# One norm pass, scale and offset in the copy, and a reordered state-space block in a twelve-block kernel

## What is computed

```python
# L1_attn: causal attention with one head
y = layer_norm(x, gamma, beta)          # x is already _layernorm(x)
q, k, v = split(y @ qkv)
p = softmax(causal(q @ k.T / 16))
out = x + (p @ v) @ o_proj

# L3_attn: a state-space layer (512 inner features, 8 heads of 64, state 128)
u_n = layer_norm(u, ln_w, ln_b)
z, x, B, C, dt = split(u_n @ in_proj_w.T)
B, C = rms_norm(B, bnorm_w), rms_norm(C, cnorm_w)
dA = softplus(dt + dt_bias) * -exp(A_log)
y = sum over s <= t of (C[t] . B[s]) * exp(cumsum(dA)[t] - cumsum(dA)[s]) * x[s]   # per head
y = (y + x * D) * silu(z)
out = u + y @ out_proj_w.T
```

## Time and profile before

| | us |
|---|---|
| median of 3 runs | 1470.83 (1466.35 to 1474.09) |
| the profiled execution | 1467.78 |
| its span, first to last instruction | 1466.0 |
| TensorE busy | 1247.5 (85%) |
| VectorE busy | 1132.9 (77%) |
| ScalarE busy | 897.5 (61%) |
| mean granted TensorE clock | 0.940 |

### The profile page before, as it was taken

One profiled execution on the slowest core, in us unless ns is written; L12 is line 12 of the kernel. 1 busy time (PEld: TensorE's weight loads), 2 busy tenths in 40 slices (PEclk: granted clock), 3 DMA queues, 4 the chain that ended last, 5 costly groups with the idle time before them and its releaser, 6 DMA issues. The chain is left out here.

```text
span 1466.0 us, 25694 instructions
## 1 busy us (share of the span) xinstructions
PE 1247.5 (85%) x9953; PEld 852.3 (58%) x9953; DVE 1132.9 (77%) x2075; ACT 897.5 (61%) x1231; POOL 303.2 (21%) x235
## 2 busy tenths in 40 slices
PE   4999998555887899867989999978797999998777
PEld 1677776442334555545756766754684766766444
DVE  6787785588787999937588898955897898897563
ACT  4777776622566787823267777744694777676423
POOL 0000000100241111000005155230461155165020
PEclk9999999887898999977999999999899999999889
DMA  6899997102005999985159998931563899987500
GB/s 241 156 173 188 183 168 124 58 2 99 1 1 101 187 193 187 196 186 137 43 110 196 179 194 168 172 116 34 190 195 90 165 176 180 169 158 128 106 1 8
DMA packets 548297, 196.41 MB, mean 134 GB/s; under 512 B 534624, under 2 KB 535008, under 8 KB 546912
## 3 DMA queue, kind: packets, MB, share of 16 engines
q1 hardware_dynamic: 548192, 195.00, 66.2%
HBM read 60.48 MB, written 0.26 MB: 41 GB/s over the span
## 5 line engine op out<-in xcount | busy, mean ns | idle before, releaser
L654 DVE SCALAR_TENSOR_TENSOR arena<-L_xattn_sm,L_xattn_rr,arena 128x1024 f16<-128x1024 f32 x192 | 278.6, 1491 | 12.1 <-ACT arena L545 12.1
L408 PE MATMUL ps<-ctxT,L_xattn_qk 128*128 128x512 f16 x1152 | 266.2, 381 | 1.9 <-DVE L_xattn_qk L621 1.4
L530 ACT ACTIVATE L_xattn_sm<-L_xattn_sm,L_xattn_mx 128x2048 f32<-128x2048 f32 x96 | 192.3, 2003 | 80.9 <-DVE L_xattn_mx L636 79.7
L545 ACT ACTIVATE arena<-L_xattn_sm,L_xattn_rr 128x1024 f16<-128x1024 f32 x192 | 210.0, 1141 | 5.2
L420 PE MATMUL ps<-arena,ctx 128*128 128x128 f16 x2976 | 188.9, 224 | 20.4 <-DMA arena<-arena 20.4
L420 PEld LDWEIGHTS ps<-arena,ctx 128*128 128x128 f16 x2976 | 177.2, 100 | 35.9 <-DMA arena<-arena 25.3
L408 PEld LDWEIGHTS ps<-ctxT,L_xattn_qk 128*128 128x128 f16 x1152 | 111.2, 98 | 128.4 <-issue 3.8
L636 DVE CUSTOM_DVE_ANT_0 L_xattn_sm<-ps,L_xattn_bias 128x1024 f32<-128x1024 f32 x96 | 117.1, 1220 | 69.2 <-issue 68.9
L636 DVE CUSTOM_DVE_ANT_0 L_xattn_sm<-ps,L_xattn_bias,L_xattn_mx 128x1024 f32<-128x1024 f32 x96 | 123.2, 1283 | 0.8 <-DVE L_xattn_mx L636 0.5
L430 PEld LDWEIGHTS ps<-arena,ctx 128*128 128x128 f16 x1488 | 90.7, 98 | 17.3 <-DMA arena<-arena 0.2
L430 PE MATMUL ps<-arena,ctx 128*128 128x128 f16 x1488 | 98.3, 219 | 0.0
(11 more groups left out here) (534 smaller groups left out, 2148.9 us busy)
## 6 DMA issues: line engine op xcount, KB each, us to landing
L_ffn_ring<-in_L_ffn_experts SPq DMA_DIRECT2D x34, 384.0 KB, 3.5
arena<-in_L_xattn_w SPq DMA_DIRECT2D x36, 320.0 KB, 3.9
arena<-in_L_ffn_experts SPq DMA_DIRECT2D x8, 768.0 KB, 8.6
arena<-in_L_xattn_w SPq DMA_DIRECT2D x6, 640.0 KB, 11.6
arena<-arena SPq DMA_TRANSPOSE x193, 4.5
arena<-in_L_ffn_codes SPq DMA_DIRECT2D x1, 3072.0 KB, 14.2
arena<-in_L_ffn_scales SPq DMA_DIRECT2D x8, 384.0 KB, 24.5
arena<-in_L_attn_w SPq DMA_DIRECT2D x1, 2163.0 KB, 8.8
```

What stands on the lines that cost most here:

```text
L408: last = nc.tensor.matmul(ps[:, at, :], qk[:, h // 2, qp, h % 2, b * P:(b + 1) * P], k.ctxT[:, cp, b, at * 512:(at + 1) * 512], start=(a = ...
L530: nc.scalar.activation(sm[:, u % 2, :], sm[:, u % 2, :], ACT.Exp, bias=mx[:, u % 2, 1:2], scale=-1.0, accum_out=rs[:, u % 2:u % 2 + 1]).th ...
L545: nc.scalar.mul(pp[:, u % 2, 0, at], sm[:, u % 2, at], rr[:, u % 2:u % 2 + 1]).then_inc(s.p_high, 1)
L654: nc.vector.scalar_tensor_tensor(pp[:, u % 2, 1, at], sm[:, u % 2, at], rr[:, u % 2:u % 2 + 1], pp[:, u % 2, 0, at], ALU.mult, ALU.subtrac ...
```

## The change

In both layers the two norms become one pass. The norm of a normed input has the same direction, and its variance follows from the first: with variance v, the two root arguments are v + eps and v(1 + eps) + eps * eps. `ln_twice_vector` takes the statistics once, both roots at once, and writes `twice` first and `once` after it. Scale and offset are held as columns and put into the copy out of PSUM on ScalarE, one activation per 128 features. The causal layer gets more fillers and an early small Exp, which brings the table load forward.

In the state-space layer the projections come in another order: B, C and steps of both batch elements first, then x, and later the gate z and x again in turned form (features on partitions). The squares go to ScalarE. The softplus is written out, with one operation less. The decay rows come ahead of the B/C transposes. The values are made in turned form, so that y is not turned and copied. D and silu(z) are applied in turned form.

```diff
+def ln_twice_vector(k, dve, x, once, twice, eps, n):
+    nc, g = k.nc, k.g
+    chain = Chain(dve, g.dve_chain, k.dve_n)
+    moments(k, dve, chain, x)
+    nc.vector.tensor_scalar(k.rstd[:, 0, :], k.mv[:, :, 1], eps, None, ALU.add)
+    nc.vector.tensor_scalar(k.rstd[:, 1, :], k.mv[:, :, 1], 1.0 + eps, eps * eps, ALU.mult, ALU.add)\
+        .then_inc(g.var_ready, 1)
+    dve.wait_ge(g.std_ready, n + 1)
+    chain(nc.vector.reciprocal(k.rstd[:], k.std[:]))
+    for out, which in ((twice, 1), (once, 0)):
+        for b in range(B):
+            last = nc.vector.tensor_scalar(out[:, b, :], x[:, b, :], k.mv[:, b, 0:1], k.rstd[:, which, b:b + 1],
+                                           ALU.subtract, ALU.mult)
...
 @@ causal_layer, TensorE @@
-                keep_busy(k, 1, 12)
-                pe.wait_ge(s.y_ready, 1)
+                keep_busy(k, 1, 13)
+                pe.wait_ge(g.xn_ready, n + 1)
...
+                keep_busy(k, 7, 4)
                 wait_weights(k, pe, slot, loaded)
-                pe.wait_ge(s.yT_ready, 1)
+                pe.wait_ge(s.yT_ready, DC)
...
-                keep_busy(k, 7, 8)
+                keep_busy(k, 7, 12)
                 pe.wait_ge(s.p_ready, 1)
...
+                keep_busy(k, 1, 2)
                 pe.wait_ge(s.pT_ready, 1)
...
+                keep_busy(k, 1, 3)
                 pe.wait_ge(s.o_ready, 1)
@@ causal_layer, ScalarE @@
-                nc.scalar.copy(flat(yT[:]), ps[:, 0, :]).then_inc(s.yT_ready, 1)
+                for c in range(DC):
+                    nc.scalar.activation(yT[:, c, :], ps[:, 0, c * T:(c + 1) * T], ACT.Identity,
+                                         bias=beta[:, c:c + 1], scale=gamma[:, c:c + 1]).then_inc(s.yT_ready, 1)
+                nc.scalar.activation(unused[:], k.zero[:], ACT.Exp, bias=k.zero[:])
@@ ssd_layer, TensorE @@
-                keep_busy(k, 7, 14)
-                pe.wait_ge(s.u_ready, 1)
+                keep_busy(k, 7, 13)
+                pe.wait_ge(g.xn_ready, n + 1)
...
+                keep_busy(k, 7, 4)
                 wait_weights(k, pe, slot, loaded)
+                pe.wait_ge(s.uT_ready, DC)
+                for b in range(B):
+                    for c in range(DC):
+                        last = nc.tensor.matmul(ps[:, 1 + b, 0:2 * SN + SH], uT[:, c, b * P:(b + 1) * P],
+                                                w_in[:, c, 2 * SI:], start=(c == 0), stop=(c == DC - 1))
+                last.then_inc(s.bc_psum, 1)
+                for b in range(B):
+                    for c in range(DC):
+                        last = nc.tensor.matmul(ps[:, 3 + b, :], uT[:, c, b * P:(b + 1) * P], w_in[:, c, SI:2 * SI],
+                                                start=(c == 0), stop=(c == DC - 1))
+                    last.then_inc(s.x_psum, 1)
+
+                def features(out, first, sem):
+
+                    for f in range(2):
+                        at = first + f * P
                         for c in range(DC):
+                            last = nc.tensor.matmul(out[:, f, :], w_in[:, c, at:at + P], uT[:, c, :],
+                                                    start=(c == 0), stop=(c == DC - 1))
+                    last.then_inc(sem, 1)
+
+                keep_busy(k, 7, 2)
                 pe.wait_ge(s.dA_ready, 1)
                 nc.tensor.matmul(ps[:, 0, 0:B * SH], k.upper[:], dA[:].rearrange("p b h -> p (b h)"),
                                  start=True, stop=True).then_inc(s.cum_psum, 1)
+
+                for b in range(B):
+                    pe.wait_ge(s.dAw_ready, b + 1)
+                    if b:
+                        pe.wait_ge(s.x_ready, B)
+                    for h in range(SH):
+                        last = nc.tensor.matmul(ROWS[b][:, h, :], dAw[:, b, h, :], k.upper[:], start=True, stop=True)
+                    last.then_inc(s.cumrow_psum, 1)
+                pe.wait_ge(s.bc_ready, 1)
...
+                for half in range(2):
+                    features(ZT[:, 2 * half:2 * half + 2, :], 2 * half * P, s.z_psum)
+                pe.wait_ge(s.bcT_ready, 2)
...
+                features(XT[0], SI, s.xT_psum)
+                pe.wait_ge(s.gm_ready, 1)
+                features(XT[1], SI + 2 * P, s.xT_psum)
+                for b in range(B):
+                    keep_busy(k, 5 + b, 6 - 3 * b)
                     pe.wait_ge(s.m_ready, b + 1)
                     for h in range(SH):
-                        last = nc.tensor.matmul(ps[:, 1 + b, h * SP_:(h + 1) * SP_], lm[:, b, h, :],
-                                                xv[:, b, h * SP_:(h + 1) * SP_], start=True, stop=True)
+                        j = SP_ * (h % 2)
+                        last = nc.tensor.matmul(Y[b][j:j + SP_, h // 2, :], xv[:, b, h * SP_:(h + 1) * SP_],
+                                                lm[:, b, h, :], start=True, stop=True, skip_group_check=True)
                     last.then_inc(s.y_psum, 1)
                 for b in range(B):
+                    keep_busy(k, 4, 5 - 3 * b)
                     pe.wait_ge(s.y_ready, b + 1)
+                    for c in range(FC):
+                        last = nc.tensor.matmul(ps[:, 3 + b, 0:D], yT[:, b, c, :], w_out[:, c, :],
+                                                start=(c == 0), stop=(c == FC - 1))
                     last.then_inc(s.out_psum, 1)
@@ LAYERS @@
-    4: (causal_layer, "L1_attn", ("L1_attn_w", "L1_attn_rows")),
+    4: (causal_layer, "L1_attn", ("L1_attn_w",)),
-    10: (ssd_layer, "L3_attn", ("L3_attn_w", "L3_attn_rows")),
+    10: (ssd_layer, "L3_attn", ("L3_attn_w", "L3_attn_cols", "L3_attn_rows")),
```

More of the change, by code:

```diff
@@ L113, in begin, with moments @@
     return k
+def moments(k, dve, chain, x):
+    for b in range(B):
+        last = k.nc.vector.bn_stats(k.stats[:, b, :], x[:, b, :])
+    chain(last)
+    for b in range(B):
+        last = k.nc.vector.bn_aggr(k.mv[:, b, :], k.stats[:, b, :])
+    chain(last)
 def ln_vector(k, dve, x, out, eps, n):
@@ L121, in ln_vector @@
     chain = Chain(dve, g.dve_chain, k.dve_n)
+    moments(k, dve, chain, x)
+    nc.vector.tensor_scalar(k.rstd[:, 0, :], k.mv[:, :, 1], eps, None, ALU.add).then_inc(g.var_ready, 1)
+    dve.wait_ge(g.std_ready, n + 1)
+    chain(nc.vector.reciprocal(k.rstd[:, 0, :], k.std[:, 0, :]))
     for b in range(B):
[L123 to L132, removed]
+        last = nc.vector.tensor_scalar(out[:, b, :], x[:, b, :], k.mv[:, b, 0:1], k.rstd[:, 0, b:b + 1],
                                        ALU.subtract, ALU.mult)
@@ new lines, in _ @@
+                pe.wait_ge(s.bc_ready, 1)
+                for j in range(2):
+                    for b in range(B):
+                        last = nc.tensor.transpose(ps[:, 7, (2 * j + b) * P:(2 * j + b + 1) * P], bcv[:, b, j, :],
+                                                   k.ident[:])
+                last.then_inc(s.bcT_psum, 1)
+                for half in range(2):
+                    features(ZT[:, 2 * half:2 * half + 2, :], 2 * half * P, s.z_psum)
+                pe.wait_ge(s.bcT_ready, 2)
@@ L2677, in _ @@
                 for b in range(B):
-                    act.wait_ge(s.zx_psum, b + 1)
-                    nc.scalar.activation(sz[:, b, :], ps[:, 3 + b, :], ACT.Silu, bias=k.zero[:]).then_inc(s.z_ready, 1)
-                    nc.scalar.copy(xv[:, b, :], ps[:, 5 + b, :]).then_inc(s.x_ready, 1)
+                    act.wait_ge(s.x_psum, b + 1)
+                    nc.scalar.copy(xv[:, b, :], ps[:, 3 + b, :]).then_inc(s.x_ready, 1)
+                for b in range(B):
+                    for j in range(2):
+                        last = nc.scalar.activation(sq[:, 2 * b + j, :], ps[:, 1 + b, j * SN:(j + 1) * SN], ACT.Square,
+                                                    bias=k.zero[:], accum_out=ms[:, b, j:j + 1])
@@ L2681, in _ @@
+                last.then_inc(s.ms_raw, 1)
+                act.wait_ge(s.ms_ready, 1)
+                nc.scalar.activation(ms[:], ms[:], ACT.Sqrt, bias=k.zero[:]).then_inc(s.rms_ready, 1)
+                nc.scalar.activation(unused[:], k.zero[:], ACT.Exp, bias=k.zero[:])
                 act.wait_ge(s.bcT_psum, 1)
-                nc.scalar.copy(bcT[:].rearrange("p b j t -> p (b j t)"), ps[:, 7, :]).then_inc(s.bcT_ready, 1)
-                for b in range(B):
+                for j, w in enumerate((bn_w, cn_w)):
+                    nc.scalar.activation(bcT[:, j, :, :], ps[:, 7, 2 * j * P:2 * (j + 1) * P]
+                                         .rearrange("p (b t) -> p b t", b=B), ACT.Copy, scale=w).then_inc(s.bcT_ready, 1)
@@ new lines, in _ @@
+                decays(1)
+                act.wait_ge(s.xT_psum, 2)
+                for f in range(2, FC):
+                    last = nc.scalar.mul(xdT[:, f, :], XT[1][:, f - 2, :], dcol[:, f:f + 1])
+                last.then_inc(s.xT_ready, 1)
+                for half in range(2):
+                    act.wait_ge(s.z_psum, half + 1)
```

(2 more changed lines are left out.)

223 lines of the change are left out of this document (93 added, 130 removed).

## The result

| | before | after |
|---|---|---|
| median, first comparison (4 runs each) | 1470.47 us | 1449.99 us (1445.9 to 1454.83) |
| ratio to the kernel before, 95% interval | | 0.987 [0.984, 0.990] |
| second comparison (run e5 below: 11 runs before, 6 after) | 1468.81 us | 1452.69 us, ratio 0.989 [0.986, 0.992] |
| profiled execution, its span | 1467.78, 1466.0 us | 1447.01, 1445.3 us |

The change makes the kernel some 20 us faster in the first comparison and 16 us in the second. I had forecast 10 us (1461, range 1454.5 to 1467), so the sign is right, the size is too small, and the measured time lies outside the range.

The account below looks back on a forecast made before the run. No engine is full; TensorE, the busiest, waits and runs partly at the low clock. Causal half 0, state-space half 9.8 us off the profiled 1467.78 gives 1458; the median lies 3 us above: 1461 us, range 1454.5 to 1467.

Parts of the forecast that it names:

- The causal half at 0: Causal block: its gain of 7.3 us is priced at 0, because the next block then waits longer for the fp4 scales.
- the case of a high start: Causal block: TensorE priced at the higher clock level throughout, with the block ending near 658.8 instead of 666.03 us.
- Rival B: Causal and fp4 blocks: the causal gain of 7.3 us arrives, 1453.7 us; chance 0.07.
- Rival C: fp4 block: earlier loads share the DMA engines and the scales land up to 9 us later, 1470 us; chance 0.05.
- Gain 9.8 us: State-space block: TensorE's work, followed in nine steps, ends at 1391.1 instead of 1400.86 us.
- rival A: State-space second half: clock falls again, 2.5 us lost, and value products cost 2.2 us more, 1465.7 us; chance 0.19.
- I take the decay records' value: State-space values: a 64-column value record priced at 0.12 us, between 0.107 and 0.19.
- Step 1: State-space head: 13 fillers, about nine slow, hold TensorE until 1359.3, so the head gives 1.95 us, not 4.
- Nothing takes this gain back: Block after the state-space one (fp8_layer): starts 9.8 us sooner, its weights in long before, so the gain stays.
- D: State-space block: TensorE gets only the low clock throughout, 29 us more, 1490 us; chance 0.04.
- E: State-space block: ScalarE pays 1.28 us more for each of two table loads before B and C, 1463.6 us; chance 0.03.
- The remark on starts: TensorE: the number of slow matmuls at a start differs between runs of one kernel, which one trace cannot show.

Follow-up runs that it names:

- e5: The changed kernel once more with no edit, for a second trace and time; 1452.69 us, ratio 0.989 to the kernel before.
- e2: The changed kernel with the old state-space layer and its old loads, so the causal half alone; ratio 1.0003 to the kernel before.
- e8: The changed kernel without the 16 fillers ahead of the value and output products; ratio 0.9872 to the kernel before.
- e10: The changed kernel with the fp4 scales laid out for 128 partitions and loaded as one wide transfer; ratio 0.9818 to the kernel before.
- e1: The kernel before once more with no edit, for a second trace; ratio 1.0015.
- e9: The kernel before with the fp4 scales laid out for 128 partitions and loaded as one wide transfer; ratio 0.9973.
- e3: The changed kernel with the old causal layer and its old loads, so the state-space half alone; ratio 0.9893 to the kernel before.
- e4: The changed kernel with the two dropped broadcast loads of rows back, into columns nobody reads; ratio 0.9893 to the kernel before.
- e6: The changed kernel with all value products of a batch written to the first 64 partitions; ratio 0.9902 to the kernel before.
- e7: The changed kernel with 7 fillers instead of 13 at the head of both blocks; ratio 0.9894 to the kernel before.
- e12: The changed kernel with wide scales, 7 fillers at both heads and none ahead of value and output products; 1439.41 us, ratio 0.981.

## Why the prediction was wrong in size

**The causal half at 0: right.** e2 is the half alone: 1.0003. The block got 5.5 us shorter (7.3 forecast for the case of a high start; it was 6.4 to 7.2 in e5 and e8, which had one), the wait for the scales grew from 2.4 us to 5.4 to 10.6 us, and e10 gives the 5.5 us back as soon as the scales land early. Rival B (the causal gain arrives) is out, though the measured time lies nearer to its 1453.7 than to my 1461. Rival C is out too: with the new causal block the next block's loads are issued earlier, and the slowest scales land 30.6 to 34.0 us after their issue (32.2 on average in seven traces), against 32.3 to 33.1 (32.8 on average in four) with the old one.

**"Gain 9.8 us" in the state-space block: the step that failed.** By the blocks it is 48.8 (mean of before, e1, e2, e9) less 34.1 (mean of after, e3, e4, e5, e10), 14.7 us. The order and the overlaps of the sum were right; three of its sizes were not, the end from which I subtracted, the price of a value record, and the start. The 4.9 us that are missing in my sum lie there.

1. *The base, 2.0 us.* I subtracted from 1400.86, the end in one trace, in which the projections ran at the high level. The three other traces of the same code lasted 48.9 to 50.0 us. In e1 the projections take 10.60 instead of 8.91 us, the decay records 6.08 instead of 4.90 and the outputs 4.42 instead of 3.62; the values take 4.71 instead of 6.02. So the old block loses time to the low level in all four traces, in the first in other records than in the three others, and the one trace that I had was the shortest. I had seen its loss from 1390 to 1395, and used it only as a risk for the new block (rival A), not as a part of the old block's time that changes between executions.
2. *The value records, 1.7 us.* "I take the decay records' value", 0.12 us, with bounds of 0.107 and 0.19. They cost 0.068. The bound from below left out that two heads are written to different halves; with one half e6 has my 0.12 us back and a block longer by 1.7 us. My lower bound had a reason (columns at the high level) that is no bound for two records at once.
3. *The start, 1.0 us on average.* Step 1, "one less ends at 1359.3", is right to 0.15 us where the block starts low (e3), and 1.8 us too late where it starts high, which makes the block 1.7 us shorter, in three of the five traces of the new block. The same code starts either way, and no run shows what decides it.

The remainder is 0.2 us. From 14.7 us for the blocks to the 16 and 20 us of the two comparisons there is a rest. It lies inside the second interval (0.986 to 0.992 is 12 to 21 us) and at the edge of the first (0.984 to 0.990 is 15 to 24 us). The 4.9 us by which untouched blocks ahead of the causal one are shorter in the traces (see e1) could fill it; their cause is open.

**"Nothing takes this gain back": right.** From the start of `fp8_layer` to the last instruction it is 64.9 us on average in the four traces of the old state-space block (63.6 to 67.7) and 64.9 in the five of the new one (63.9 to 65.9).

**Rivals A, D and E.** A asked for a fall of the clock in the second half: in all seven traces with the late fillers (after, e3 to e7, e10) a window from the projections to the last output has the clock at 1.00; e12, without them, shows a fall. D falls with it. E: B and C are transposed 16.9 us after the start in e3 (17.0 forecast), with both loads in front of them. The 1.38 us of drain that the Trainium skill (ScalarE: Activation LUTs, What ACT_TABLE_LOAD costs) adds to each load of a table doesn't show at these two. In the timeline of the changed kernel Ln and Sqrt start 0.01 and 0.02 us behind loads of 1.28 us:

```profile
1355.66 1.28 ACT L2704 ACT_TABLE_LOAD   x1
1356.95 0.31 ACT L2704 ACTIVATE L_attn_tl<-L_attn_te,ones 128x16 f32<-128x16 f32 x1
...
1360.22 1.28 ACT L2714 ACT_TABLE_LOAD   x1
1361.52 0.30 ACT L2714 ACTIVATE L_attn_ms<-L_attn_ms,zero 128x4 f32<-128x4 f32 x1
```

**The remark on starts held.** What I cited against certainty in rival A, from the Trainium skill (TensorE: Matmul & The Clock Gate, Part 1), the number of slow matmuls at a start that changes between runs of one kernel, is what the traces show: 13 fillers at the head of the state-space block took 2.97 us in the first trace of the changed kernel and 4.65 in its second (e5).

## What to carry to other kernels

Before a gain is subtracted from a block's time, see at which clock each of its long records ran; if some ran low, the block has other lengths in other executions, and a change that removes its pauses can remove that loss too. A speedup ahead of a transfer that already ends a wait is worth nothing until the transfer is earlier: here one line of layout took 7.3 us off the two blocks with the change and 2.2 us without it. Fillers in front of a wait can cost or save: at a low start thirteen made a block 1.3 us longer than seven did (e7), and with none ahead of the last products the clock fell in one of two traces (e12, not e8).

## What the runs showed of the hardware

- Float32 products with 64-column weights whose results go to the two halves of the partitions in turn take 0.068 us a record of 128 columns (1.09 us for 16, after); all on one half they take 0.12 us (1.96 us for 16, e6).
- Eight spread transfers of 384 KB (one row to 16 partitions each) have their slowest landing 30.6 to 34.0 us after its issue, behind 3 MB of codes (eleven traces); the same bytes as one plain transfer of 3 MB, from a source sixteen times as large, land after 17.9 us (e9, e10).
- The granted clock stayed at 2.4 GHz through a wait of 1.75 us in one execution (e8) and was at 1.2 GHz behind the same wait in another (e12, 0.57 on average from 1366 to 1370).
